# Moving the stack loads to SyncE's queue, with a new order of work on ScalarE and GpSimd and other paces, in a float32 decoder layer

## The reference

```python
x = x + attention(layernorm(x))          # 32 query heads, 8 key/value heads of 32, rope, causal
x = x + cross(layernorm(x), ctx)         # fake_quant(x) @ fake_quant(ctx), 1024 x 1024
x = x + ffn(layernorm(x))
# attention: qkv = x @ w_qkv.T + b_qkv ; rope(q), rope(k) ; softmax(q k / sqrt(32)) v ; @ w_o.T + b_o
# fake_quant(x) = (clip(round(x / s + z), 0, 255) - z) * s
# ffn: base = x @ W_org.T ; coeffs = softmax(keys of (mean over tokens of x) @ Wq)   (8 experts)
#      h = x @ lora_down[e] (rank 64) ; delta = sum_e coeffs[e] * h[e] @ lora_up[e] ; base + delta
```

## Time and profile before

| | us |
|---|---|
| median of 3 runs | 702.71 (701.38 to 705.21) |
| the profiled execution, its own time | 701.59 |
| its span, first to last instruction | 699.8 |
| busy in the span: PE, DVE, ACT, POOL | 651.6, 427.6, 423.0, 283.2 |
| mean granted TensorE clock | 0.985 of full speed |

### The profile page before, as it was taken

One profiled execution on the slowest core, in us unless ns is written; L12 is line 12 of the kernel. 1 busy time (PEld: TensorE's weight loads), 2 busy tenths in 40 slices (PEclk: granted clock), 3 DMA queues, 4 the chain that ended last, 5 costly groups with the idle time before them and its releaser, 6 DMA issues.

```text
span 699.8 us, 12690 instructions
## 1 busy us (share of the span) xinstructions
PE 651.6 (93%) x4512; PEld 527.5 (75%) x4512; DVE 427.6 (61%) x1127; ACT 423.0 (60%) x1025; POOL 283.2 (40%) x317
## 2 busy tenths in 40 slices
PE   4996899999999899999889799899999999899998
PEld 3985677888877678888666577688777778688886
DVE  6795777876877734665886965533144899821122
ACT  5425678878778847679968685756233793720310
POOL 2047645534444263347320540515634205943520
PEclk9999999999999999999997989999999999999999
DMA  7648854752455523323663341313434363433102
GB/s 261 241 140 243 237 143 127 218 147 76 140 152 172 174 103 110 121 58 95 181 183 123 87 119 30 112 40 89 153 120 143 129 204 128 152 123 103 46 25 95
DMA packets 43934, 93.47 MB, mean 134 GB/s; under 512 B 5504, under 2 KB 5888, under 8 KB 42432
## 3 DMA queue, kind: packets, MB, share of 16 engines
q1 hardware_dynamic: 34416, 66.45, 29.4%
q0 software_dynamic: 3696, 15.73, 9.4%
q10 hardware_dynamic: 5760, 10.49, 4.1%
HBM read 72.72 MB, written 19.92 MB: 132 GB/s over the span
## 4 chain that ended last, share of the span: by engine, by line
PE 68%; DVE 12%; ACT 7%; issue 5%; POOL 5%; DMA 2%; ACTq 0%; DVEq 0%
PE dense L1092 33%; PE score L1092 8%; PE probt L980 8%; PE pv L996 5%; PE score L968 5%; PE pv L1092 3%; POOL w_lo L1715 2%; ACT prob_all L1186 2%; DVE stats L1389 2%; DVE xres L1493 2%; ACT w_hi L1139 1%; PE misc L1005 1%; DVE prob_all L1344 1%; DVE w_lo L1324 1%; PE misc L1035 1%
## 5 line engine op out<-in xcount | busy, mean ns | idle before, releaser
L1344 DVE CUSTOM_DVE_ANT_0 prob_all<-score,mask_sb 128x128 f32<-128x128 f32 (+3 forms) x256 | 123.2, 488 | 115.9 <-PE score L968 114.3
L1715 POOL TENSOR_TENSOR w_lo<-stage,w_hi 128x512 fp32r<-128x512 f32 x85 | 109.9, 1302 | 194.7 <-ACT w_hi L1139 194.3
L1092 PE MATMUL dense<-w_hi,act_t 128*128 128x512 f32 (+1 forms) x536 | 180.1, 390 | 7.5 <-POOL w_lo L1715 2.5
L1186 ACT ACTIVATE prob_all<-prob_all,neg_max 128x128 f32<-128x128 f32 (+3 forms) x256 | 142.7, 558 | 36.6 <-DVE neg_max L1344 34.9
L1092 PE MATMUL dense<-act_t,w_hi 128*128 128x512 f32 x366 | 123.2, 418 | 1.3 <-POOL w_lo L1715 1.2
L980 PE MATMUL probt<-ident_sb,prob_all 128*128 128x128 f32 x640 | 115.0, 279 | 5.6 <-ACT prob_all L1195 3.5
L1092 PEld LDWEIGHTS dense<-w_hi,act_t 128*128 128x128 f32 x536 | 100.2, 193 | 24.6 <-POOL w_lo L1715 4.5
L1092 PE MATMUL dense<-w_lo,act_t 128*128 128x512 f32 (+1 forms) x298 | 107.6, 379 | 0.7 <-ACT w_lo L1144 0.3
L980 PEld LDWEIGHTS probt<-ident_sb,prob_all 128*128 128x128 f32 x640 | 80.2, 143 | 24.7 <-issue 9.3
L1139 ACT ACTIVATE w_hi<-stage 128x512 fp32r<-128x512 f32 x117 | 72.1, 623 | 44.0 <-PE dense L1092 18.4
L1195 ACT ACTIVATE prob_all<-probt 128x128 f32<-128x128 f32 (+3 forms) x160 | 68.6, 429 | 48.2 <-PE probt L980 46.7
(11 more groups left out here) (204 smaller groups left out, 1011.1 us busy)
## 6 DMA issues: line engine op xcount, KB each, us to landing
q_stack<-rope_dram POOLq DMA_DIRECT2D x15, 768.0 KB, 7.1
stage<-in_w_qk SPq DMA_DIRECT2D x40, 256.0 KB, 2.9
rope_dram<-act_t ACTq DMA_DIRECT2D x40, 256.0 KB, 2.8
stage<-in_w_o SPq DMA_DIRECT2D x32, 256.0 KB, 2.9
stage<-in_ctx_kv SPq DMA_DIRECT2D x24, 256.0 KB, 3.3
stage<-in_w_org SPq DMA_DIRECT2D x24, 256.0 KB, 3.3
xres<-in_x SPq DMA_DIRECT2D x8, 512.0 KB, 5.9
prob_all<-in_x SPq DMA_DIRECT2D x8, 512.0 KB, 6.2
```

Source lines behind the costliest of these rows:

```text
L1092: last = engine.matmul(dst, lhs, rhs, start=(k == 0 and c == 0), stop=(k == g.kts - 1 and c == len(pairs) - 1))
L1186: engine.activation(prob[:, u % P_SLOTS, 0:length], prob[:, u % P_SLOTS, 0:length], ACT.Exp, bias=neg_max[:, m:m + 1], scale=-1.0, accum_o ...
L1344: engine.tensor_tensor_reduce(prob[:, u % P_SLOTS, 0:length], score_bank[u % 2][:, 0:length], mask_sb[:, S - length:S], -1.0, HIGHEST, ALU ...
L1715: engine.tensor_tensor(slot_lo(p, 0, NW), raw_of(p), slot_hi(p, 0, NW).bitcast(F32), ALU.subtract).then_inc(g_piece, 1)
```

## The change

Five edits. The loads of all stacks are issued by SP, in each slot after `put_roped` and before `fetch`, with the same waits; POOL issues no DMA any more. ACT makes the rope's high part before the units (u < 0) after the tokens' high parts of the slot, and no longer before them. `on_vector` leaves all low parts of `base(0)`, half 0, to POOL. `PACES` has new entries around `cross(0)` and `base(0)`. The bias of sequence 1 is added in the slot in which the fifth step of its `out` tile is due.

```diff
-    PACES = [(("out", 0, 0), 0.55), (("down", 0, 0), 1.15), (("out", 1, 0), 1.0)]
+    PACES = [(("out", 0, 0), 0.55), (("cross", 0, 0), 1.15), (("base", 0, 0), 1.6), (("down", 0, 0), 1.1), (("out", 1, 0), 1.0)]
@@ on_vector
-        return p < 8 and p % 2 == 1 or piece["kind"] == "q" and piece["b"] == 0 and piece["nb"] < 4 or piece["kind"] == "out" and p % 2 == 1 or piece["kind"] == "base" and piece["b"] == 0 and piece["nb"] == 0 and p % 2 == 1
+        return p < 8 and p % 2 == 1 or piece["kind"] == "q" and piece["b"] == 0 and piece["nb"] < 4 or piece["kind"] == "out" and p % 2 == 1
@@ sync_program: new, and taken out of gpsimd_program in the same form
+            def load_stacks(gi):
+                b, g = divmod(gi, NKV)
+                mk, mq = plan.rope_no["k", b, g // GROUP], plan.rope_no["q", b, g]
+                if gi >= 2:
+                    e.wait_ge(t_score, last_unit(gi - 2) + 1)
+                e.wait_ge(*roped(mk))
+                rows = rope_dram[mk].rearrange("a (r h) c -> h r a c", h=GROUP)[g % GROUP]
+                engine.dma_start(k_stack[0:TERMS * HD, gi % 2, :].bitcast(F32), rows).then_inc(d_kstack[gi % 2], 16)
+                e.wait_ge(*roped(mq))
+                rows = rope_dram[mq].rearrange("a (r h) c -> r a (h c)", h=GROUP)
+                engine.dma_start(q_stack[0:TERMS * HD, gi % 2, :, :].rearrange("p h c -> p (h c)").bitcast(F32),
+                                 rows).then_inc(d_qstack[gi % 2], 16)
...
@@ sync_program, walk through the slots
                 for m in rope_out_at.get(j, ()):
                     put_roped(m)
+                if j == first_queries_at:
+                    load_first_keys()
+                    for pair in range(GROUP // 2):
+                        load_first_queries(pair)
+                for gi in load_at.get(j, ()):
+                    load_stacks(gi)
                 for p in at["fetch"].get(j, ()):
                     fetch(p)
@@ scalar_program
                 for m in rope_high_at.get(j - 1, ()):
                     put_high(m)
-                for m in rope_high_at.get(j, ()):
-                    rope_high(m)
+                if u >= 0:
+                    for m in rope_high_at.get(j, ()):
+                        rope_high(m)
...
                 for halves in at["turn"].get(j, ()):
                     tokens_high(*halves)
+                if u < 0:
+                    for m in rope_high_at.get(j, ()):
+                        rope_high(m)
@@ gpsimd_program
-                if j == first_queries_at:
-                    load_first_keys()
-                    for pair in range(GROUP // 2):
-                        load_first_queries(pair)
-                for gi in load_at.get(j, ()):
-                    load_stacks(gi)
...
-                if NT <= biased < B * NT and u >= UNITS + 8 + 2 * (biased - NT):
+                if NT <= biased < B * NT and u >= UNITS + 8 and j >= plan.slot_of[plan.begin["out", 1, 0, biased - NT]] + 4:
                     add_output_bias(1, biased - NT)
```

More of the change, by code:

```diff
@@ L796, in load_second, with load_first_keys, load_first_queries @@
                 engine.dma_start(x_second[:, t, :], x[1, t * P:(t + 1) * P, :]).then_inc(d_xb[t], 16)
+            def load_stacks(gi):
[10 more added lines that the diff above has]
+                                 rows).then_inc(d_qstack[gi % 2], 16)
+            def load_first_keys():
+                m = plan.rope_no["k", 0, 0]
+                e.wait_ge(*roped(m))
+                rows = rope_dram[m].rearrange("a (r h) c -> h r a c", h=GROUP)[0]
+                engine.dma_start(k_stack[0:TERMS * HD, 0, :].bitcast(F32), rows).then_inc(d_kstack[0], 16)
+            def load_first_queries(pair):
+                m, heads = plan.rope_no["q", 0, 0], slice(2 * pair, 2 * pair + 2)
+                e.wait_ge(*roped(m))
+                rows = rope_dram[m].rearrange("a (r h) c -> r a h c", h=GROUP)[:, :, heads, :].rearrange("r a h c -> r a (h c)")
+                engine.dma_start(q_stack[0:TERMS * HD, 0, heads, :].rearrange("p h c -> p (h c)").bitcast(F32),
+                                 rows).then_inc(d_qfirst[pair], 16)
             def fetch(p):
@@ L1670, in rope_low @@
                 engine.tensor_tensor(r["raw"].bitcast(F32R), r["raw"], r["high"].bitcast(F32), ALU.subtract).then_inc(g_rlo, 1)
[L1672 to L1688, removed]
-                engine.dma_start(k_stack[0:TERMS * HD, 0, :], rows.bitcast(F32R)).then_inc(d_kstack[0], 16)
-            def load_first_queries(pair):
-                m, heads = plan.rope_no["q", 0, 0], slice(2 * pair, 2 * pair + 2)
-                e.wait_ge(*roped(m))
-                rows = rope_dram[m].rearrange("a (r h) c -> r a h c", h=GROUP)[:, :, heads, :].rearrange("r a h c -> r a (h c)")
-                engine.dma_start(q_stack[0:TERMS * HD, 0, heads, :].rearrange("p h c -> p (h c)"),
-                                 rows.bitcast(F32R)).then_inc(d_qfirst[pair], 16)
             def ln(instruction):
```

## The result

The changed kernel takes **709.0 us** (median of 6 runs, 705.84 to 711.38); the kernel before takes 702.96 in the same comparison. The ratio is 1.0078, 95% interval 1.0046 to 1.0110: slower by 0.8%, where 699.8 was forecast. The profiled execution took 710.42 us with a span of 707.5.

The account below looks back on a forecast made before the run. PE's work, its gaps (48 us in all) and work at the lower clock were taken as the bound. Terms of -1.9, -0.3 and -0.7 summed to -2.9 us, from 702.71 to 699.8 us; range 694.5 to 704.5.

Parts of the forecast that it names:

- Low parts of base(0), half 0: Near 400 us: a DVE low part at 398.87 leaves the chain, -0.7 us; POOL's added low parts stay hidden.
- Paces: 0, the same work for PE either way: Around cross(0) and base(0): new paces shift steps between slots, PE's work unchanged; 0, bounds -1 and +1 us.
- Head: -1.9: Before about 80 us: loads off POOL and ScalarE's new order shorten the start by 1.9 us, bounds -0.5 to -3.2.
- The other loads leave POOL: -0.3: Later stack loads: the one at 329.30 us goes some 9 us sooner from SP; -0.3 us, bounds 0 and -1.7.
- the prediction's own rival for SP's queue: SP's list: a stack load ahead of fetches holds them up, at most 3.3 us, one fetch's landing; bound +2.
- SP's queue as the new wait: 0: SP's list: fetches and put_roped wait behind stack loads, but SP seldom comes early; 0, bound +2 us.
- Bias of sequence 1: 0: Four adds of 2.4 us move from 496 to 505 us to beside out(1); 0, at most +0.6 us.
- C: Rival, chance 0.16: slower, 706.4 to 707.7 us, as the piece-starved stretch lengthens at low clock, again near 400 us.
- B: Rival, chance 0.17: the head gives nothing, or the DVE saving turns into POOL waits; 702.5 us, within 1.5 of before.
- PE waiting for POOL's low parts at 400 to 415: Sign of being wrong: between 400 and 415 us PE waits for low parts made by POOL.
- a mean clock below 0.98 in 340 to 420: Sign of being wrong: the mean granted clock from 340 to 420 us is below 0.98.

Follow-up runs that it names:

- e6: The changed kernel with POOL's low part of the fourth base(0) piece moved ahead of the fourth norm chain; 703.84 us, ratio 1.0025 to the kernel before.
- c1: The changed kernel with three odd low parts of base(0), half 0, back on DVE and the first left on POOL; 699.34 us, ratio 0.9952 to before.
- e7: The changed kernel with DVE's last scaling ahead of the routing and POOL's low part ahead of the fourth norm chain; 700.13 us, ratio 0.9965 to before.
- e1: The changed kernel with the odd low parts of base(0), half 0, back on DVE; 699.28 us, ratio 0.9935 to the kernel before.
- g2: The changed kernel with the odd low parts of base(0), half 0, back on DVE, measured a second time; 699.40 us, ratio 0.9960 to before.
- e3: The changed kernel with the old paces and the odd low parts of base(0), half 0, back on DVE; 702.22 us, ratio 0.9990 to before.
- e2: The changed kernel with the old paces, low parts still on POOL; 706.46 us, ratio 1.0040 to the kernel before.
- c3: The changed kernel with the odd low parts on DVE and the bias adds at their old place; 698.84 us, ratio 0.9953 to before.
- e4: The changed kernel with base at pace 1.15 again and cross still at 1.6, low parts on POOL; 705.55 us, ratio 1.0023 to before.

## Why the prediction was wrong

**The step that failed: "Low parts of base(0), half 0", priced -0.7, "hidden ... Uncovered it would be +1.3 per piece on PE, at most 2 pieces".** One piece was uncovered, and it was not 1.3 but 2.27 us late, since what lay ahead of it was not the low part's own 1.27 us but a whole norm chain, 404.89 to 407.7. The prediction saw that POOL "makes the first new one behind the third of four norm chains" and argued that the chains are not urgent; it did not ask the reverse, what the pieces lose behind the fourth one. The trace of before would have shown it: POOL was in that chain from 405.25 to 408.1, and PE took up the piece's step at 407.31.

```profile
405.25 0.19 POOL L878 TENSOR_SCALAR ln_s<-mean_var 128x1 f32<-128x1 f32 x1
...
407.82 0.26 POOL L897 TENSOR_SCALAR ln_s<-mean_var,ln_s 128x1 f32<-128x1 f32 x1
```
```profile
407.31 0.48 PE L1092 MATMUL dense<-w_hi,act_t 128*128 128x512 f32 x1
407.63 0.39 PE L1092 MATMUL dense<-w_lo,act_t 128*128 128x512 f32 x1
```

The prediction also read POOL as "idle in half of each stretch or more" from 100 us on; in the stretch that mattered, 400 to 410, its own row has POOL busy in 8.00 of 10 us. Then the half clock doubled the price: the stage grew by 6.7 us from 36.16, and moving that one instruction gave 4 of them back (e6). The other 2.7 are not traced to a single wait. What was right in the step is the -0.7 on the chain at 398.87: PE's wait there was 1.93 for 2.27, and 1.49 with just that piece on POOL and the other three on DVE (c1).

The Trainium skill's "GPSIMD Engine Reference", section "Performance versus the Vector engine", has GpSimd at about half VectorE's rate for a two-input elementwise operation. The trace agrees (1274 against 691 ns), but e7 shows that the rate is not what made the kernel slower: with the same 89 low parts on POOL, in another order, the kernel is faster than before.

**"Paces: 0, the same work for PE either way"** failed in both directions, with bounds of 1 us. With DVE's low parts they gain 2 to 4 us, by e1, g2 and e3; with POOL's they lose 2.7 by the ratios of the changed kernel and e2. The work is the same, but which slot an instruction falls into decides what stands ahead of it on another engine. I counted slots (40 for 38) and took only the length from it, not the meeting in slot 302.

**"Head: -1.9".** The places came out as forecast: no gap over 1 us between 66 and 70, unit 0 scored at 71.32, landing of the stacks 6.5 us, below 7. The size did not: 0.7 in the first pair of profiles, 0.8 on average. The forecast had POOL's add end at 72.3. It ended at 73.04, since ScalarE's high part for the low part ahead of it was ready at 70.45 and not at 69.6, behind a normalising and the tokens' high part:

```profile
68.21 1.23 ACT L1197 ACTIVATE prob_all<-prob_all,ln_s 128x1024 f32<-128x1024 f32 x1
69.34 0.59 ACT L1251 ACTIVATE act_t<-probt 128x512 fp32r<-128x512 f32 x1
69.82 0.63 ACT L1171 ACTIVATE w_hi<-stage 128x512 fp32r<-128x512 f32 x1
```
```profile
70.52 1.28 POOL L1725 TENSOR_TENSOR w_lo<-stage,w_hi 128x512 fp32r<-128x512 f32 x1 [0.81 <-ACT w_hi L1171]
71.76 1.28 POOL L1701 TENSOR_TENSOR xres<-xres 128x512 f32<-128x512 f32 x1
```

So the gap that had ended at 80.53 ended at 79.36 and not at 78.6, 1.2 us sooner than before; group 1 started 0.7 sooner, and the rest went at the lower clock between the two. Averaged over the profiles with both parts of the new head, that gap ends 1.7 us sooner, near the forecast, and group 1 starts 0.8 sooner. The sum had no term for the clock in the head, since the row of before stood at 1.00.

**"The other loads leave POOL: -0.3".** The load that was to go 9 us sooner went at 329.54, for 329.30 before: in SP's list it stands behind the fetches of three context pieces, issued from 322.29 to 329.5 as their buffers came free. That is the prediction's own rival for SP's queue the other way round, a fetch holding up a load. Nothing came of it, and no loss either.

**"SP's queue as the new wait: 0"** held: fetches landed in 2.8 to 3.1 us at the median, before in 2.9 to 3.3, and e3 is not slower than before. The median hides two: the fetches issued right behind the first stacks, at 65.8 and 68.5 us, took 8.55 and 6.86 us to land (before, none near there took over 4.5), and no engine waited for them. The rule of the Trainium skill's "DMA: Bandwidth & Descriptors", section "SWDGE vs HWDGE vs iDMA", was weighed in the prediction, with 3.4 us for a fetch behind a stack. Those two fetches go with it, 5.7 and 4.0 us over the median of 2.85, but no run here shows such a fetch making PE wait.

**"Bias of sequence 1: 0"** held: c3 against e1, and the stage from first store to end is 132.4 us in both kernels.

**The rivals.** C named the right place and came within 1.3 to 2.6 us of the 709.0: low clock "a second time, near 400, while POOL is behind with its low parts between four norm chains", 706.4 to 707.7; it had a chance of 0.16 as its case against was "the freed steps are only one slot's worth", an argument about `cross`, which had no part in the loss (42.58 us from group 13 to 14 with the old paces in e2, 42.88 with the new `cross` alone in e4). It missed the second loss at 499.6, so the nearness of its total is in part luck. B was right for the head alone. Of the signs of being wrong, "PE waiting for POOL's low parts at 400 to 415" told; "a mean clock below 0.98 in 340 to 420" could not, as it is 0.87 in the changed kernel and was 0.89 before.

## What to carry to other kernels

Before an instruction moves to another engine's list, read what will stand *ahead* of it there at the moment when its reader needs it; its own length may be the smaller part of the price (here 1.27 us, for a chain of 2.8). When a pace or a slot count changes, list the pairs of instructions that newly share a slot on an in-order engine, for an instruction that waits (here routing for weighing) holds up ready work behind it. And a gap of 2 us on TensorE is to be priced with the half clock that can follow: here 4.05 us for one of 2.27, though e7's gap of 1.78 was followed by none.

## What was not expected of the hardware

The granted clock differs between executions of the same program. The stretch from group 1 to 11, in which all these kernels do the same work in the same slots, took 226.3 to 227.9 us in 19 of the 20 profiles (224.8 in e4). One window sorts them: from 240 to 255 us the granted clock is 1.00 in e4, 0.89 in the nine profiles of 226.3 to 226.8 us, and 0.77 in the ten of 227.4 to 227.9; the kernel before is in both groups. And three profiles of the kernel before show 1.00, 1.00 and 0.83 from 75 to 85 us. Over 35 runs of the kernel before on one chip the time went from 698.72 us (mean clock 0.992) to 707.40 (0.975), with a correlation of -0.85 between time and clock (-0.61 to -0.79 in the other comparisons). In one pair of profiles a difference of 1 us in one stage is therefore no evidence; where a stage is averaged above, it is over profiles that share the edit in question.
